# Two-layer gated cross-attention: scores computed by row tiles of TensorE, two heads at a time

## The reference, cut to what matters

```
q = (ln(x) @ Wq.T + bq)         # [256, depth] per head
k = (ctx @ Wk.T + bk)           # [512, depth] per head
scores = q @ k.T / sqrt(depth)  # [256, 512]
out = softmax(mask(scores)) @ v
```

## Time and profile before

| | us |
|---|---|
| median of 3 runs | 332.14 (330.86 to 333.17) |
| the profiled execution | 330.76 |
| its span, first to last instruction | 328.9 |

### The profile page before, as it was taken

The page is one execution under the profiler, slowest core; times in us unless marked ns, Lnnn a source line. Parts: engine busy times, 40 slices in busy tenths (PEclk is TensorE's granted clock), DMA queues, the critical chain, the costliest instruction groups (busy, mean ns, idle before and its releaser), DMA issues.

```text
span 328.9 us, 6642 instructions
## 1 busy us (share of the span) xinstructions
PE 292.6 (89%) x1963; PEld 211.9 (64%) x1963; DVE 256.7 (78%) x775; ACT 225.6 (69%) x523; POOL 117.1 (36%) x185
## 2 busy tenths in 40 slices
PE   2759899998869798989979999999989989979996
PEld 0546577666546475657646666776757667957995
DVE  1589888788795999999879999999799507566554
ACT  1259698778675989997879998888787532432221
POOL 4346687676463343353123333223323300000000
PEclk9979999999998999999999999999999999999999
DMA  5991000000000000000000000000000000000000
GB/s 162 421 413 53 3 2 2 2 0 4 0 0 2 1 3 0 2 1 2 1 2 1 2 0 2 2 2 1 2 1 1 2 2 0 0 1 18 0 2 16
DMA packets 3603, 9.30 MB, mean 28 GB/s; under 512 B 625, under 2 KB 2289, under 8 KB 3057
## 3 DMA queue, kind: packets, MB, share of 16 engines
q1 hardware_dynamic: 3136, 8.54, 6.6%
q10 hardware_dynamic: 432, 0.35, 0.5%
HBM read 8.62 MB, written 0.26 MB: 27 GB/s over the span
## 4 chain that ended last, share of the span: by engine, by line
PE 51%; DVE 23%; issue 14%; ACT 5%; POOL 3%; DMA 2%; DVEq 0%; ACTq 0%; POOLq 0%
PE bank L864 12%; PE bank L967 11%; DVE masked L614 4%; PE bank L885 4%; PE bank L1009 3%; PE bank L1029 3%; PE bank L889 3%; PE bank L1032 3%; PE bank L942 3%; PE bank L948 2%; PE bank L947 2%; DVE probsT L630 2%; DVE k_both L676 2%; PE bank L882 2%; DMA cols<-in_cols 2%
## 5 line engine op out<-in xcount | busy, mean ns | idle before, releaser
L384 POOL TENSOR_SCALAR probs<-probs,rsum 128x512 f32<-128x512 f32 x128 | 88.9, 697 | 133.6 <-DVE rsum L623 133.1
L450 ACT ACTIVATE probs<-masked,neg_max 128x512 f32<-128x512 f32 x128 | 92.1, 720 | 7.7 <-DVE neg_max L614 6.4
L614 DVE CUSTOM_DVE_ANT_0 masked<-bank,mask 128x512 f32<-128x512 f32 x128 | 87.5, 684 | 7.4 <-PE bank L942 4.9
L864 PE MATMUL bank<-ident,probs 128*128 128x128 f32 x512 | 80.2, 280 | 2.8 <-DVE probsT L630 1.6
L864 PEld LDWEIGHTS bank<-ident,probs 128*128 128x128 f32 x512 | 57.6, 141 | 31.3 <-issue 22.4
L967 PE MATMUL bank<-probsT,val 128*32 128x256 f32 (+1 forms) x512 | 52.5, 396 | 1.8 <-ACT mixT L466 1.7
L458 ACT ACTIVATE probsT<-bank 128x512 f32<-128x512 f32 x74 | 43.6, 590 | 11.9 <-PE bank L864 11.5
L630 DVE COPY probsT<-bank 128x512 f32<-128x512 f32 x54 | 36.7, 679 | 10.2 <-PE bank L864 10.2
L967 PEld LDWEIGHTS bank<-probsT,val 128*32 128x32 f32 (+1 forms) x512 | 22.9, 124 | 27.8 <-issue 16.8
L560 ACT ACTIVATE probsT<-bank 128x256 f32<-128x256 f32 x34 | 13.0, 385 | 36.3 <-PE bank L1029 36.3
L942 PE MATMUL bank<-k,q 128*128 128x512 f32 x64 | 31.7, 501 | 6.2 <-issue 5.9
(11 more groups left out here) (128 smaller groups left out, 449.0 us busy)
## 6 DMA issues: line engine op xcount, KB each, us to landing
we<-in_we SPq DMA_DIRECT2D x3, 1088.0 KB, 14.5
w1T<-in_w1T SPq DMA_DIRECT2D x1, 2048.0 KB, 10.5
w0T<-in_w0T SPq DMA_DIRECT2D x1, 768.0 KB, 7.3
ctxT<-in_ctxT SPq DMA_DIRECT2D x2, 256.0 KB, 5.8
bv<-in_L_xattn_b_V SPq DMA_DIRECT2D x1, 512.0 KB, 10.6
x_sb<-in_x SPq DMA_DIRECT2D x2, 128.0 KB, 5.6
w0T<-in_w0T ACTq DMA_DIRECT2D x1, 256.0 KB, 4.5
m_u<-in_mask SPq DMA_DIRECT2D x1, 256.0 KB, 6.3
```

What stands on the lines that cost most here:

```text
L384: pool.tensor_scalar(p, p, rsum[:, u % NCOL:u % NCOL + 1], 1.0, ALU.mult, ALU.mult).then_inc(normed, 1)
L450: act.activation(probs[:, u % NP, :], masked[:, u % NS, :], ACT.Exp, scale=-1.0, bias=neg_max[:, c:c + 1], accum_out=sums[:, c:c + 1]).the ...
L614: dve.tensor_tensor_reduce(out=masked[:, u % NS, :], in0=score_bank[u % 2][:, :], in1=mask, scale=-float(k.depth) ** -0.5, scalar=3.0e38, ...
L864: ins = pe.transpose(dst[0:rows, t * P:t * P + P], src, ident[:, :])
```

## The change

- Scores are computed for two units at a time, at even t only, and the two units are two heads of the same query tile. Each head is a row tile: 32 rows of the array in layer 0, 64 in layer 1. The two heads write the two score banks.
- In layer 0 one matmul of 32 rows per head. The 32 rows hold four copies of the head's 8 rows, so there is no `q_stack`, and no `stack_f`.
- In layer 1 three products per head, of 64 rows: high/high, high/low, low/high, ordered so that the two heads alternate.
- High and low keys and queries are one instruction each over 128 rows.
- PE waits until both banks are empty before it fills the pair.
- The expert spreading matrix and the transposed gates get tiles of their own, and POOL clears half of the first (64x2048) in the middle of the kernel.

```
 def unit(u):
     k = [k for k in BLOCKS if k.first <= u < k.end][0]
-    return (k, *divmod(u - k.first, NQ))
+    pair, one = divmod(u - k.first, 2)
+    both, qt = divmod(pair, NQ)
+    return k, 2 * both + one, qt
...
-            def q_stack(m):
-                pool.wait_ge(*freed(("q", m)))
-                if m >= 2:
-                    pool.wait_ge(scored, BLOCKS[m - 2].end)
-                for j in range(4):
-                    pool.tensor_scalar(q0[:, m % 2, j, :], stack_f[:, :], head_row[:, j:j + 1], 1.0,
-                                       ALU.mult, ALU.mult).then_inc(q0_ready, 1)
...
+                    publish_late(pool.memset(spread[64:P, :, :].bitcast(F32), 0.0))
...
-                    own = [slice(64 * h, 64 * h + 64) for h in range(2)]
-                    if name == "k":
-                        act.activation(k1_high[:, i, :], job_bank[:, :], ACT.Identity, bias=bias[:, row]).then_inc(high_ready, 1)
-                        act.wait_ge(high_ready, HIGHS[j])
-                        for h in range(2):
-                            act.activation(k1_both[own[1 - h], i, h, :], k1_high[own[h], i, :], ACT.Copy).then_inc(cross_ready, 1)
-                    else:
-                        for h in range(2):
-                            act.activation(q1_high[own[h], i, h, :], job_bank[own[h], 0:cols], ACT.Identity,
-                                           bias=bias[own[h], row]).then_inc(high_ready, 1)
+                    high = (q1_high, k1_high)[name == "k"]
+                    act.activation(high[:, i, :], job_bank[:, 0:cols], ACT.Identity, bias=bias[:, row]).then_inc(high_ready, 1)
...
     # on DVE, layer 1: six instructions for k and q become two
+                        low, high, bias = ((q1_low, q1_high, bq1), (k1_low, k1_high, bk1))[name == "k"]
+                        dve.scalar_tensor_tensor(out=low[:, i, :], in0=job_bank[:, 0:cols], scalar=bias[:, row],
+                                                 in1=high[:, i, :].bitcast(F32), op0=ALU.add, op1=ALU.subtract).then_inc(free, 1)
...
             def scores(u):
-                dst = score_bank[u % 2][:, :]
+                pe.wait_ge(*freed(("q", k.m)))
                 if u >= 2:
-                    pe.wait_ge(maxed, u - 1)
+                    pe.wait_ge(maxed, u)
                 if k.layer == 0:
-                    pe.wait_ge(q0_ready, 4 * k.m + h + 1)
-                    pe.matmul(dst, q0[:, i, h, q], k0[:, i, :], start=True, stop=True).then_inc(scored, 1)
+                    for one in range(2):
+                        rows = slice(32 * (h + one), 32 * (h + one) + 32)
+                        pe.matmul(score_bank[one][:, :], q0[rows, i, q], k0[rows, i, :], start=True, stop=True).then_inc(scored, 1)
                 else:
-                    pe.wait_ge(*freed(("q", k.m)))
-                    pe.wait_ge(own_ready, 2 * (k.m - 7))
-                    pe.wait_ge(cross_ready, 2 * (k.m - 7))
-                    pe.matmul(dst, q1_high[:, i, h, q], k1_high[:, i, :], start=True, stop=False)
-                    pe.matmul(dst, q1_both[:, i, h, q], k1_both[:, i, h, :], start=False, stop=True).then_inc(scored, 1)
+                    for n, (qs1, ks1) in enumerate(((q1_high, k1_high), (q1_high, k1_low), (q1_low, k1_high))):
+                        for one in range(2):
+                            rows = slice(64 * one, 64 * one + 64)
+                            ins = pe.matmul(score_bank[one][:, :], qs1[rows, i, q], ks1[rows, i, :], start=(n == 0), stop=(n == 2))
+                            if n == 2:
+                                ins.then_inc(scored, 1)
...
-                if 0 <= t + LEAD < TOTAL:
+                if 0 <= t + LEAD < TOTAL and (t + LEAD) % 2 == 0:
                     scores(t + LEAD)
```

More of the change, by code:

```diff
@@ L54 @@
 for _name, _n in (("bq0", 4), ("bk0", 4), ("bq1", 8), ("bk1", 8), ("gates", 4), ("lo_k", 1), ("lo_q", 1),
-                  ("head_row", 4), ("neg_half", 4)):
+                  ("lo_gate", 1), ("neg_half", 4)):
     COL[_name], NCOLS = slice(NCOLS, NCOLS + _n), NCOLS + _n
@@ L133, in make_plan @@
         if j[0] in ("k", "q"):
-            count += 2 if j[0] == "q" and BLOCKS[j[1]].layer == 1 else 1
+            count += 1
             highs[j] = count
@@ L181, in build @@
         lo_k, lo_q = cols[:, COL["lo_k"]], cols[:, COL["lo_q"]]
-        head_row, gates = cols[:, COL["head_row"]], cols[:, COL["gates"]]
+        lo_gate, gates = cols[:, COL["lo_gate"]], cols[:, COL["gates"]]
         bq0, bk0, bq1, bk1 = (cols[:, COL[n]] for n in ("bq0", "bk0", "bq1", "bk1"))
@@ L209, in build @@
         high_q = sb("high_q", [P, SQ], F32R)
-        stack_f = sb("stack_f", [P, SQ])
         w0T = sb("w0T", [P, 4, 4, P])
@@ L220, in build @@
         k0 = sb("k0", [P, 2, SK], F32R)
-        q0 = sb("q0", [P, 2, 4, SQ], F32R)
+        q0 = sb("q0", [P, 2, SQ], F32R)
         w1T = sb("w1T", [P, 8, 4, P])
@@ L228, in build @@
         k1_high = sb("k1_high", [P, 2, SK], F32R)
-        k1_both = sb("k1_both", [P, 2, 2, SK], F32R)
-        q1_both = sb("q1_both", [P, 2, 2, SQ], F32R)
-        q1_high = sb("q1_high", [P, 2, 2, SQ], F32R)
+        k1_low = sb("k1_low", [P, 2, SK], F32R)
+        q1_high = sb("q1_high", [P, 2, SQ], F32R)
+        q1_low = sb("q1_low", [P, 2, SQ], F32R)
         fw = sb("fw", [P, P])
@@ L265, in build @@
         gate_full = sb("gate_full", [2 * EXPERTS, SQ])
-        spread = q0[:, :, :, :].rearrange("p i h t -> p (i h t)").rearrange("p (e h) -> p e h", h=HID)
-        gateT = k0[:, 0, :]
+        spread = sb("spread", [P, EXPERTS, HID], F32R)
+        gateT = sb("gateT", [P, TOK], F32R)
         flat = probsT[:, :, :, :, :].rearrange("p a h k q -> p (a h k q)")
@@ L407, in _ @@
                     norm(t + LEAD - 3)
-                for job in PLAN.get(t - 1, ()):
-                    if job[0] == "q" and BLOCKS[job[1]].layer == 0:
-                        q_stack(job[1])
                 if t == LN01_AT + 1:
@@ L655, in job @@
                     i, row = k.m % 2, slice(k.g, k.g + 1)
+                    cols = SK if name == "k" else SQ
+                    if k.m >= 2:
+                        dve.wait_ge(scored, BLOCKS[k.m - 2].end)
+                    dve.wait_ge(high_ready, HIGHS[j])
                     if k.layer == 0:
[L658 to L665, removed]
@@ L666, in job @@
-                        cols = SK if name == "k" else SQ
-                        dve.wait_ge(high_ready, HIGHS[j])
-                        dve.scalar_tensor_tensor(out=dst, in0=job_bank[:, 0:cols], scalar=bias[:, row],
-                                                 in1=high[:, :].bitcast(F32), op0=ALU.add, op1=ALU.add).then_inc(free, 1)
[L670 to L679, removed]
-                    else:
[L681 to L688, removed]
@@ new lines, in job @@
+                        dst, high, bias = ((q0, high_q, bq0), (k0, high_k, bk0))[name == "k"]
+                        dve.scalar_tensor_tensor(out=dst[:, i, :], in0=job_bank[:, 0:cols], scalar=bias[:, row],
+                                                 in1=high[:, :].bitcast(F32), op0=ALU.add, op1=ALU.add).then_inc(free, 1)
+                    else:
+                        low, high, bias = ((q1_low, q1_high, bq1), (k1_low, k1_high, bk1))[name == "k"]
+                        dve.scalar_tensor_tensor(out=low[:, i, :], in0=job_bank[:, 0:cols], scalar=bias[:, row],
+                                                 in1=high[:, i, :].bitcast(F32), op0=ALU.add, op1=ALU.subtract).then_inc(free, 1)
@@ L766, in router @@
                 if o == 8:
-                    dve.wait_ge(late_ready, 7)
+                    dve.wait_ge(late_ready, 6)
                     dve.wait_ge(*freed(("logits", b)))
@@ L1058, in lay_out @@
     for i, n in enumerate(("L0_xattn_Wq", "L0_xattn_Wk")):
-        w = f[n].reshape(4, 32, P).transpose(2, 0, 1)
-        w0T[:, :, i, :] = np.tile(w, (1, 1, 4))
+        w = f[n].reshape(4, 4, 1, 8, P).transpose(4, 0, 1, 2, 3)
+        w0T[:, :, i, :].reshape(P, 4, 4, 4, 8)[:] = w
     w0T[:, :, 2, :].reshape(P, 4, 4, 32)[:, :, :, 0:8] = f["L0_xattn_Wv"].reshape(4, 4, 8, P).transpose(3, 0, 1, 2)
@@ L1078, in lay_out @@
     for n, w in (("bq0", "L0_xattn_bq"), ("bk0", "L0_xattn_bk")):
-        cols[:, COL[n]] = np.tile(f[w].reshape(4, 32).T, (4, 1))
+        cols[:, COL[n]] = np.tile(f[w].reshape(4, 4, 1, 8), (1, 1, 4, 1)).reshape(4, P).T
     for n, w in (("bq1", "L1_xattn_b_Q"), ("bk1", "L1_xattn_b_K")):
@@ L1083, in lay_out @@
     row = np.arange(P)
-    cols[:, COL["lo_k"]] = np.where(row // 32 % 2, -1.0, 0.0)[:, None]
-    cols[:, COL["lo_q"]] = np.where(row // 64, -1.0, 0.0)[:, None]
-    cols[:, COL["head_row"]] = (row[:, None] % 32 // 8 == np.arange(4))
+    cols[:, COL["lo_k"]] = np.where(row // 8 % 2, -1.0, 0.0)[:, None]
+    cols[:, COL["lo_q"]] = np.where(row // 16 % 2, -1.0, 0.0)[:, None]
+    cols[:, COL["lo_gate"]] = np.where(row // 32 % 2, -1.0, 0.0)[:, None]
     cols[:, COL["neg_half"]] = -0.5
```

10 lines of the change are left out of this document (1 added, 9 removed).

## The result

The changed kernel takes 340.18 us in the median of 4 runs (339.22 to 341.68), against 332.55 for the kernel before: ratio 1.0237, 95% interval 1.0204 to 1.027. The forecast was 339.0. The profiled execution took 340.26 us, its span is 338.5, so it stands 9.5 us above the profiled execution of before, somewhat more than the medians do (7.6). Some executions of the kernel before and of the variants run one or two per cent longer at a lower mean granted clock; the ratios leave these out, the medians given here do not.

What follows compares the result with a forecast made beforehand. PE was taken to bound steady layer 1, with DVE, ACT and POOL busy in layer 0 and DVE chains holding PE in the middle. Terms summed to +7.1 on 330.76, 337.9, or 339 at the median; range 326 to 350.

Steps and rivals of the forecast that it cites:

- case A: Whole kernel: row tiles overlap, each change of tiling costs 0.15 us, layer 0 pays the pair wait; 339 us, chance 0.45.
- blocks 0 and 1: First layer 0 blocks, partly held up by loads and the weight quantiser: +0.8 us each, 1.6 together.
- blocks 5 to 7: Middle stretch, 72.5 to 119.7 us: +4.8 for coupling against 5.4 saved on DVE in key and query jobs, 0 net.
- units 64 to 71: A DVE-heavy stretch, expected to take 0.7 us less.
- blocks 10 to 19: 40 units, 135.4 to 227.1 us: 17.8 per eight units plus 2.9 extra PE jobs and 2.2 chain stalls, +2.5 us.
- PE's price for a pair: Layer 1 score pair: 0.69 us passes, two switches of 0.15, 0.1 weight load; 1.09 instead of 0.93.
- The layer 0 block: Steady layer 0: the pair wait stretches a block from 11.14 to 12.8 us, 1.6 more.
- The loop through the turn: Layer 0: PE's pair waits for DVE's masking, which waits for DVE's copy of the turn behind PE's jobs and mix.
- The four hand-overs: Layer 0 block, from one pair's first ready bank to the next: 2.7, 3.6, 3.0 and 3.5 us.
- (B): Rival, mainly in PE-bound layer 1: row tiles overlap and switches cost nothing; 326 us, chance 0.25.
- (D): Rival in both layers: row tiles do not overlap, +30 us in all; 362 us, chance 0.12.
- (E): Rival in the middle stretches: DVE chains hit PE in full without run-ahead, +7 us; 347 us, chance 0.15.

Runs made afterwards that it cites:

- experiment 4: The changed kernel with the layer 1 loops exchanged, one head's three products before the other's: 340.54 us, ratio 1.0262.
- experiment 5: The changed kernel with three 128-row matmuls instead of six row-tile ones per layer 1 pair, heads not separated: 330.5 us, ratio 0.9944.
- experiment 1: The kernel before with scores of two units computed together after both banks are empty, no row tiles: 348.07 us, ratio 1.0486.
- experiment 6: Layer 0 of the kernel before with layer 1 of the changed kernel: 331.77 us, ratio 0.9954.
- experiment 3: The changed kernel with the pair of scores moved behind the jobs, mix and turn of an even step: 347.06 us, ratio 1.0473.
- Experiment 9: The changed kernel with eight extra PE transposes at each of steps -4 to 0, ahead of the pair wait: 338.28 us, ratio 1.0175.
- experiment 7: Kernel before with only layer 1 changed; there scores also move behind the even step's turn, mix half ahead of the odd step's job: 327.94 us, ratio 0.9874.
- experiment 2: The changed kernel with the pair wait split, each head's bank filled once that bank is empty: 340.29 us, ratio 1.0215.

## Why the prediction held, point by point

**Direction and size.** 339.0 forecast, 340.18 measured, by case A: tiles overlap, each change of tiling costs, and layer 0 pays the pair wait. Span against span the sum was +7.1 and is +9.5; the terms, read from the starts of the exponentials:

| term | forecast | measured |
|---|---|---|
| start | -0.6 | -0.4 |
| blocks 0 and 1 | +1.6 | +4.7 |
| blocks 2 to 4 | +4.8 | +4.8 |
| blocks 5 to 7 | 0 | +0.1 |
| units 64 to 71 | -0.7 | +0.7 |
| blocks 10 to 19 | +2.5 | +0.2 |
| tail | -0.5 | -0.4 |

That the total came within 1.2 us owes something to luck: blocks 0 and 1 and units 64 to 71 cost 4.5 more than forecast, and blocks 10 to 19 cost 2.3 less.

**PE's price for a pair** was right to 0.01 (1.10) and rests on the price of a mix in column tiles. What it is made of is shown: overlap by the timeline and experiment 4, passes no slower and 0.41 for both switches and the exposed load by experiment 5. The split within the 0.41 is not as forecast: 0.21 fall in the pair and 0.20 behind it, for 0.25 and 0.15. What of the 0.21 is the switch and what the load, no run tells.

**The layer 0 block**, 12.8 forecast and 12.8 measured, is the best-founded step: experiment 1 makes it without tiles, experiment 6 makes it go. My reason for it was only partly complete. The loop through the turn exists, but experiment 3 showed that it isn't the only one; the turn's two banks and the even spacing of the mixes matter too, by how much no run tells. The four hand-overs came out right one by one, to 0.1 us, since each was followed in the program's order, not since the one loop explains them.

**The term that was mis-sized** is blocks 0 and 1, +1.6 for +4.7. I had counted only the hand-overs. The wait behind the quantiser leaves PE idle for 3.58 us, and the lower clock after it was not in the sum. Experiment 9 gives it 2.9 us, nearly all of the 3.1 that the term is off.

**Blocks 10 to 19** came out 2.3 better. Steady units took the 17.8 of the forecast, but I had carried over 2.2 us of chain stalls on top of the extra jobs, and they did not stay: five times 17.8 and 2.9 are the 91.9 measured. In the slowest eight units PE is without work for 1.2 us (20.50 - 19.34), before for 2.4 (21.20 - 18.77). That this is DVE's relief, 67.5 us busy instead of 84.4, is argued from the busy times.

**Units 64 to 71** took 0.7 more instead of 0.7 less. I had counted DVE's relief there and left out the four pairs' price, 0.6. Experiment 5, without tiles in layer 1, has 15.6 for these units instead of 16.4.

**The rivals.** That tiles are free (B) falls with 17.8 in steady layer 1 and with experiment 5, which is that case in layer 1 alone. That they do not overlap (D) falls with the timeline. The dearer coupling in the middle (E), +7 on top, falls with 44.9 against 44.8, and even the longest of these stretches, 47.8, is only 3.0 above. The forecast zero is right no closer than that spread. That DVE's and POOL's relief there balances the wait is argued, not shown: the wait alone (experiment 1) has 47.6 in those three blocks (86.0 to 133.6) at the same mean clock of 0.96, and the change's other parts take back 2.7 of it. Two of the rivals' sums are off without bearing on the result: E's terms give 346, not 347, and D's +30 is its matmuls alone (24 and 6), without the coupling that the text counts in.

**What the change is made of.** The pair wait costs 16.2 us (experiment 1), all else in the change gives about 8 back, and with layer 0 as it was, without the pair wait and without tiles, the kernel is level with before.

## What to carry to other kernels

Before two results are computed together to save matmul passes, ask what their banks did apart: two banks filled in turn are a unit of run-ahead, and filling both at once spends it; the price shows where the two engines are near balance (layer 0), not where one of them is full (steady layer 1). Count two changes of tiling for each group of tiled matmuls, and place tiled groups of different kinds next to each other. Look at the start, where the pipeline is thin, for gaps that a new wait makes long enough to cost TensorE its clock.

## What the runs showed of the hardware

- Two 64-row tiles overlap in full, and a tile's passes cost what full ones do (0.23 for 512 columns in one pass). They overlap also when three matmuls of one tile stand ahead of the other's in the program (experiment 4), so alternating them by hand buys nothing. The Trainium skill, TensorE: Matmul & The Clock Gate, section Part 3: Packing small matmuls — row/col tiling, says that matmuls never leave program order in start or end; the trace of experiment 4, with each form of the two heads at once, does not fit that, unless the program's order was changed on its way to the engine.
- A direct change from row to column tiles costs 0.15, as much as one from full mode (experiment 7: a mix behind a pair takes 1.01, as behind any other group).
- In the trace of experiment 4 the granted clock reads full all through the start, but the v group takes 2.08 instead of 1.16, as in the changed kernel; in that of experiment 2 it is the same. The durations of a known group say more than that row. The row of experiment 4's page, and the group:

```profile
PEclk9999999999999899999999999999999999999999
```
```profile
22.41 2.08 PE L843 MATMUL bank<-w0T,ctxT 128*128 128x128 f32 x8
```
